# Cross attention of a decoder layer: halves prepared outside the items, value products in two passes

## The reference, cut to what matters

```python
x = layernorm(x + attn(x, W_K, W_Q, W_V, W_O))        # 16 heads, causal
x = layernorm(x + xattn(x, ctx, ctx, gamma))          # this is the stage that changes
x = layernorm(x + ffn(x, W_g, W_u, W_d))              # ternary weights

def xattn(q, k, v, gamma):        # all (4, 512, 512); 8 heads of 64 rows of the second axis
    qh, kh, vh = (t.reshape(B, 8, 64, 512) for t in (q, k, v))
    qk = einsum('bhdq,bhdl->bhql', qh, kh) / sqrt(64)
    sm = softmax(qk, axis=-1)
    return gamma * einsum('bhql,bhdl->bhdq', sm, vh).reshape(B, 512, 512)
```

## Time and profile before

| | us |
|---|---|
| median of 3 runs | 1504.17 |
| lowest and highest | 1502.49, 1505.21 |
| the profiled execution, its own time | 1502.57 |
| its span, from first to last instruction | 1500.8 |
| TensorE busy | 1434.7 (96%) |
| VectorE busy | 1100.5 (73%) |
| ScalarE busy | 725.1 (48%) |
| GpSimd busy | 636.6 (42%) |

### The profile page before, as it was taken

How to read it: one execution, slowest core, us unless ns; L and a number is a source line. 1 busy time by engine, 2 the same in 40 slices (tenths; PEclk the granted TensorE clock), 3 DMA queues, 4 the chain that set the end, 5 groups by cost and what they waited for, 6 DMA issues and landing times. The chain is left out here.

```text
span 1500.8 us, 24088 instructions
## 1 busy us (share of the span) xinstructions
PE 1434.7 (96%) x6988; PEld 1146.6 (76%) x7008; DVE 1100.5 (73%) x2368; ACT 725.1 (48%) x1549; POOL 636.6 (42%) x493
## 2 busy tenths in 40 slices
PE   7999999999999999999999999859999989999996
PEld 5788888888888888888888888737887765565564
DVE  4667677776777676777767776678999995796854
ACT  3444444545444444444353544438987863323332
POOL 1333424334243334242433433357887853343432
PEclk9999999999999999999999999979999999999998
DMA  6566666666656666666666664811224103000000
GB/s 175 155 166 169 167 169 163 167 161 166 161 164 160 161 161 171 167 165 164 162 167 158 168 166 133 210 50 54 60 60 151 36 1 112 1 29 28 0 29 28
DMA packets 193609, 185.09 MB, mean 123 GB/s; under 512 B 97057, under 2 KB 170785, under 8 KB 193313
## 3 DMA queue, kind: packets, MB, share of 16 engines
q1 hardware_dynamic: 192416, 184.09, 45.7%
q10 hardware_dynamic: 1152, 0.52, 0.2%
HBM read 113.25 MB, written 71.30 MB: 123 GB/s over the span
## 5 line engine op out<-in xcount | busy, mean ns | idle before, releaser
L583 ACT ACTIVATE probs<-probs,neg_max 128x128 f32<-128x128 f32 (+3 forms) x256 | 142.5, 557 | 357.8 <-DVE neg_max L707 350.2
L411 POOL TENSOR_TENSOR v_lo<-placed,v_hi 128x512 fp32r<-128x512 f32 x64 | 83.2, 1299 | 366.1 <-ACT v_hi L589 366.1
L413 POOL TENSOR_TENSOR pT_lo<-placed,pT_hi 128x1280 fp32r<-128x1280 f32 x64 | 189.2, 2956 | 0.0
L767 DVE SCALAR_TENSOR_TENSOR acc<-attn_bank,prob_recip,acc 128x512 f32<-128x512 f32 x256 | 174.8, 745 | 8.1 <-PE attn_bank L483 3.3
L1303 POOL TENSOR_TENSOR prod_lo<-prod,prod_hi 128x512 fp32r<-128x512 f32 x64 | 84.7, 1323 | 143.2 <-ACT prod_hi L1412 143.2
L707 DVE CUSTOM_DVE_ANT_0 probs<-attn_bank,mask 128x128 f32<-128x128 f32 (+3 forms) x256 | 117.2, 481 | 8.3
L682 DVE TENSOR_TENSOR qT_lo<-attn_bank,qT_hi 128x512 fp32r<-128x512 f32 x64 | 44.2, 691 | 105.2 <-ACT qT_hi L571 105.2
L950 POOL TENSOR_SCALAR xprobs<-xprobs,xprob_recip 128x512 f32<-128x512 f32 x128 | 99.9, 797 | 36.1 <-DVE xprob_recip L1130 36.0
L719 DVE STREAM_TRANSPOSE turned<-probs 128x256 f32<-128x256 f32 (+1 forms) x384 | 113.9, 362 | 0.0
L1362 PE MATMUL y_bank<-wdT_f32r,prod_hi 128*128 128x512 f32 x256 | 110.7, 432 | 2.3 <-POOL prod_lo L1303 1.8
L483 PE MATMUL attn_bank<-woT_hi,zT_hi 128*128 128x512 f32 x256 | 101.2, 395 | 8.9 <-DVE zT_lo L682 8.9
(11 more groups left out here) (145 smaller groups left out, 3887.5 us busy)
## 6 DMA issues: line engine op xcount, KB each, us to landing
turned_scratch<-turned SPq DMA_DIRECT2D x64, 896.0 KB, 3.9
placed<-turned_scratch SPq DMA_DIRECT2D x256, 224.0 KB, 4.3
rows_twice<-in_ctx_dram SPq DMA_DIRECT2D x64, 128.0 KB, 2.6
acc<-in_x_dram SPq DMA_DIRECT2D x16, 256.0 KB, 5.2
rows<-in_L_attn_W_V_dram SPq DMA_DIRECT2D x64, 64.0 KB, 2.3
rows<-in_L_attn_W_O_dram SPq DMA_DIRECT2D x64, 64.0 KB, 2.7
rows_twice<-in_L_ffn_W_g_dram SPq DMA_DIRECT2D x64, 64.0 KB, 3.1
rows_twice<-in_L_ffn_W_u_dram SPq DMA_DIRECT2D x64, 64.0 KB, 2.0
```

The source lines that it names most:

```text
L413: nc.gpsimd.tensor_tensor(pT[par][1][:], placed_probs, pT[par][0][:].bitcast(F32), ALU.subtract).then_inc(p_lo, 1)
L583: nc.scalar.activation(probs[:, cols], probs[:, cols], ACT.Exp, bias=low[:, par, t:t + 1], scale=-1.0, accum_out=total[:, par, t:t + 1]).t ...
L767: nc.vector.scalar_tensor_tensor(out=acc[:, b * NT + t, :], in0=s_bank[t][:], scalar=recip[:, b, t:t + 1], in1=acc[:, b * NT + t, :], op0= ...
```

## The change

In attention, the context is split into halves ahead of its use. At the end of each head's loop (step 3) SyncE loads one of the sixteen context tiles, GpSimd scales it by one eighth (`XSCALE`) and makes its high and low part (`split`, three operations of 512 columns), and SyncE writes both to DRAM (`keep_halves`, 512 KB). The load of `wu` moves from step 0 to step 1, since the tile shares a slot with it. For the last head, `split` stands in GpSimd's queue between the last `halves_lo` and the two norm powers, and SyncE waits for the last write before the stage ends.

In cross attention, SyncE loads ready halves for item m + 4 (two DMAs of 256 KB, `load_halves`). The halves of `x` are made once for a pair: ScalarE takes the high part of the 128 rows in unit 1 of even items, GpSimd the low part, and SyncE copies them from `rows_pair` into `xs` with two DMAs of 128 KB for each item. GpSimd's `split_context` and VectorE's `xs` operation are gone.

The value product of a unit is two matmuls. `val` holds five blocks of 64 columns for each pair: low of item 0, high of item 0, zeros, high of item 1, low of item 1. For item 0 the weights are (low, high) against the high probabilities and (high, zeros) against the low ones, for item 1 (high, low) and (zeros, high). So each item has a bank of its own: 64 rows hold high values by high probabilities, or with it high by low, and the other 64 the remaining part. Both must be scaled by gamma and added: ScalarE takes one half of the bank into `z_gamma` (`main_part`), VectorE adds the other (`rest`), both for each item, in unit 1 of the next item (for h = 7 at the item's end). GpSimd's addition of a pair now stands behind the scaling of the next even item, and for the last pair of a batch in item 7.

```diff
+    def load_halves(self, sp, cp, b, h):
+        for side in range(2):
+            sp.dma_start(cp[h % 2][side * XD:(side + 1) * XD, :, :],
+                         self.kept[bass.ds(b, 1), h * XD:(h + 1) * XD, :, :].rearrange("o r k d -> (o r) k d")).then_inc(self.halves_loaded[h % 2], 16)
...
                     if b == 3:
                         keep_signs(h, 0)
+                        wait_apart(sp, k, f_turn, h * 3 + 3)
+                        rows.load_split_tile(sp, h)
...
                     if b == 3:
                         keep_signs(h, 1)
                         keep_signs(h, 2)
+                        rows.keep_halves(sp, halves, k, h)
...
                 for b in range(1, B):
                     halves_lo(FIRST + b, b % 2)
+                rows.split(nc, pool, halves, k, H - 1)
                 for b in range(2):
                     norm_gpsimd(nc, pool, norm, k.minus_half, b)
...
-                    nb, nh = ahead(b, h, 6)
-                    if exists(m + 6, ITEMS) and exists(m + 4, ITEMS):
-                        wait_count(sp, cp_ready, m + 5)
-                        source.load_twice(sp, nb, nh)
+                    nb, nh = ahead(b, h, 4)
+                    if exists(m + 4, ITEMS):
+                        if exists(m + 2, ITEMS):
+                            wait_apart(sp, k, scores_full, m * NT + 3 * NT)
+                        source.load_halves(sp, cp, nb, nh)
+                        rows = slice(nh % 2 * XD, (nh % 2 + 1) * XD)
+                        if nh % 2 == 0:
+                            wait_apart(sp, k, x_lo, nb * PAIRS + (nh // 2 + 1))
+                        for part in range(2):
+                            sp.dma_start(xs[nh % 2][part * XD:(part + 1) * XD, :].bitcast(F32),
+                                         x_parts[rows, part, :]).then_inc(xs_loaded[nh % 2], 16)
                     if is_item(b, h, B - 2, 0):
                         signs.load(sp)
...
+                def pairs_to_add(b, h):
+                    pair = h // 2 - 1 if h % 2 == 0 else PAIRS - 1 if h == XH - 1 else -1
+                    return [pair] if pair >= 0 and exists(b * XH + 2 * pair, ITEMS - 2) else []
...
                             nc.gpsimd.tensor_scalar(probs[q][:, t, :], probs[q][:, t, :], recip[:, q, t:t + 1], 1.0,
                                                     ALU.mult, ALU.mult).then_inc(probs_ready, 1)
-                    if pair_ends(b, h):
-                        pool.wait_ge(z_scaled, b * PAIRS + (h // 2 + 3))
-                        tile = acc[:, bass.ds(b * NT + h // 2, 1), :].rearrange("p o d -> p (o d)")
+                    for pair in pairs_to_add(b, h):
+                        wait_apart(pool, k, z_scaled, b * XH + (2 * pair + 4))
+                        tile = acc[:, bass.ds(b * NT + pair, 1), :].rearrange("p o d -> p (o d)")
                         nc.gpsimd.tensor_tensor(tile, z_gamma[:], tile, ALU.add).then_inc(z_added, 1)
...
-                            for n, (vp, pp) in enumerate(SPLIT):
-                                lt = nc.tensor.matmul(z_bank[pair % 2][:], val[vp][:, j, pair, 2 * par:2 * par + 2, :].rearrange("p a d -> p (a d)"),
-                                                      pT[pp][:, j, :], start=(par == 0 and j == 0 and n == 0),
-                                                      stop=(par == 1 and j == NT - 1 and n == 2))
+                            for pp, slot in enumerate(((0, 1), (3, 2))[par]):
+                                lt = nc.tensor.matmul(z_bank[par][:], val[:, j, pair, slot:slot + 2, :].rearrange("p a d -> p (a d)"),
+                                                      pT[pp][:, j, :], start=(j == 0 and pp == 0), stop=(j == NT - 1 and pp == 1))
...
+                def main_part(b, h, j):
+                    g = z_turn(b, h, j)
+                    if g is None or not exists(b * XH + g, ITEMS - 2):
+                        return
+                    own, other = z_rows(g)
+                    act.wait_ge(z_full, b * XH + (g + 1))
+                    if g % 2 == 0:
+                        act.wait_ge(z_added, b * PAIRS + (g // 2 + 1))
+                    nc.scalar.activation(z_gamma[own, :], z_bank[g % 2][other, :], ACT.Copy, scale=source.gamma[other, 0:1]).then_inc(z_main, 1)
...
+                def rest(b, h, j):
...
+                    dve.wait_ge(z_main, b * XH + (g + 1))
+                    nc.vector.scalar_tensor_tensor(out=z_gamma[own, :], in0=z_bank[g % 2][own, :], scalar=source.gamma[own, 0:1],
+                                                   in1=z_gamma[own, :], op0=ALU.mult, op1=ALU.add).then_inc(z_scaled, 1)
...
+                def last_pair(g):
...
-                dve.wait_ge(z_full, B * PAIRS)
-                tile = acc[:, B * NT - 1, :]
-                nc.vector.scalar_tensor_tensor(out=tile, in0=z_bank[(PAIRS - 1) % 2][:], scalar=source.gamma[:, 0:1], in1=tile,
-                                               op0=ALU.mult, op1=ALU.add).then_inc(z_added, 1)
+                for g in (XH - 2, XH - 1):
+                    last_pair(g)
```

155 lines of the change are left out of this document (93 added, 62 removed).

## The result

| kernel | median us | lowest to highest | ratio to before, 95% |
|---|---|---|---|
| before | 1504.2 | 1502.5 to 1505.2 | |
| after | 1543.4 | 1539.9 to 1546.6 | 1.0264, 1.0245 to 1.0282 |

A forecast was written before the change was run, and what follows sets the result against it. TensorE bounds attention; in cross attention TensorE, VectorE and ScalarE stand close together, and VectorE becomes the bound. Terms for batches, stage ends, signs and start sum to +31.5 us on 1502.6, 1534.1, for the median 1536; range 1518 to 1556.

The forecast's parts named there:

- The bound of a pair: Cross attention: TensorE falls from 13.4 to 11.6 us, VectorE binds at 11.9; with 0.5 for hand-overs, 12.4 without waits.
- rival D: Value products: the two remaining matmuls take longer than two of three did, so no cut; no chance of its own.
- The wait for the addition: Cross attention: one z_gamma buffer makes VectorE's rest wait 3.0 us for GpSimd, eleven times; such pairs take 15.4.
- Rival A: Cross attention: no wait for GpSimd's addition, which ends before ScalarE's turn; 1502 us, faster than before; chance 0.12.
- The clock: Cross attention: TensorE's clock held in most waits, at nothing in the sum; up to six falls within the range.
- rival B: Cross attention: TensorE's clock falls in each of eleven waits, 1.7 us each, +19, 1555 us; chance 0.17.
- The signs: Items 16 to 18: loads for item 21 land behind the 4 MB, TensorE waits; +3.4 us, from 0 to 6.
- Batch 2: Cross attention: waits plus a norm no longer partly hidden behind the bound VectorE; 65.0 us against 58.0, +7.0.
- Batch 3: Cross attention, VectorE already the bound: two waits partly filled by norm operations, 2 x 1.2, and one rest more; +3.0 us.
- End of attention: Last head: GpSimd's split ahead of batch 0's norm power delays VectorE; +2.9 us, 0 if the engine behind has slack.
- Start of the cross stage: First scores wait for GpSimd's low part and a DMA of xs; +2.0 us, between 0 and 4.
- Rival C: Cross attention: a transfer late in every item, 28 items x 0.5 us on top of the forecast, 1550; chance 0.06.

The follow-up runs named there:

- two buffers: The changed kernel with a second z_gamma buffer, so a pair's first product waits for the addition of the pair before the last: 1513.2 us, 1.0066.
- the experiment with the addition first: The changed kernel with one z_gamma, GpSimd adding the pair ahead of its four scalings of the even item instead of behind them: 1513.0 us, 1.0059.
- the busy wait: The changed kernel with TensorE repeating a unit's transposes six times in items 3, 5 and 7 of each batch, so it hardly idles: 1537.2 us, 1.0222.
- the pieces: The changed kernel with the two 2 MB loads of signs at item 16 made eight of 512 KB, one an item from 16 to 23: 1540.3 us.
- all repairs: The changed kernel with a second z_gamma, signs in eight loads, end-of-attention edits, item 0's query cast earlier, last pair's main parts on ScalarE with one addition: 1504.8 us, 1.0005.
- the halves alone: The changed kernel's split, kept and loaded context and query halves, with value products and z as in the kernel before: 1512.7 us, 1.0059.
- the experiment on the end of attention: The changed kernel with the last context tile's split behind the first norm power and the last W_u load ahead of batch 2's exchange: 1544.1 us.

## Why the prediction was right, and where its sum was not

The forecast was 1536, with 1518 to 1556; 1543.4 came, 7 above it. The sign, the mechanism and its place were right. That the sum came as near as it did is in part luck, as the end of this list shows.

- **Attention loop**, nothing: right. TensorE is busy for 440 of 440 us beside 176 GB/s.
- **The bound of a pair**: TensorE's 11.6 and VectorE's 11.9 stand. The hand-overs were put at 0.5 and are 0.9 (12.8 in the first pair and, with two buffers, in all). The step left ScalarE out, which needs 12.4 by its pitch and is the nearest of the three. Value matmuls still start 0.23 apart, so rival D had nothing in it.
- **The wait for the addition**: the mechanism, its place and the count of eleven were right, and taking it away by a buffer or by GpSimd's order gives 30 us. Its size was 2.3, not 3.0: the addition ended 4.3 us behind the reciprocal, not 4.7, because the four scalings take 2.70 where the earlier trace rows had 3.12, and VectorE came to `rest` 2.75 behind it, not 2.6. Rival A didn't come; it would have needed the order of the experiment with the addition first, and even there the time was 1513, not 1502.
- **The clock** is the term that was mis-sized most. The sum put it at nothing, "the clock held in most", with up to six falls in its own range. Six waits of eleven were followed by half clock in the profiled execution, and the busy wait gave 6 us back, about four falls, in the median. So the truth lay between the forecast and rival B, which had all eleven. A pair with a fall is 12.8 + 2.3 + 1.6 = 16.7, one without it 15.1, where 15.4 was forecast. The price, 1.7 against 1.6, was right by luck: it took a fall of 6.8 us and half of its loss hidden by TensorE's slack; the fall lasts 3.4 us, and of the 1.7 us of work that it loses almost nothing was hidden. And the bracket, 2.94 us left alone and 4.14 followed by a fall, was drawn from two gaps of the attention stage. The trace of before had a third, the 2.64 us ahead of the first scores in the earlier trace rows, at the start of the stage, where TensorE had had little to do. Behind that one the clock fell:

```profile
996.60:997.20 0.60, 0.60 (x3) 0.51 (x4) 0.00 (x0) 0.00 (x0) 0.60 (x1) 1.00 0.64 140
997.20:1000.00 2.80, 2.80 (x9) 1.50 (x7) 2.42 (x4) 1.84 (x4) 2.80 (x3) 0.51 0.49 140
```

The Trainium skill, "TensorE: Matmul & The Clock Gate", section "A second HAM failure mode: psum-queue depth-cycling", which the prediction weighed, tells of short idle times that make the clock swing; the cross stage agrees with it, at 0.93 granted over 1036 to 1150 us, against 1.00 both with two buffers and with the busy wait.
- **The signs**: the mechanism was right, the term too small: 3.4 was put down, within 0 to 6, and the pieces gave 5.9 to 6.2 back.
- **Batch 2**: its norm was put down in full, 7.2, since VectorE is the bound. With all repairs, so without the waits, the falls and the 4 MB in one go, batch 2 takes 55.0, which is 3.8 more than four pairs of 12.8. About half of the norm is hidden after all: a pair of 12.8 leaves VectorE, at 11.9, some room.
- **Batch 3**: 3.0 was forecast, 1.4 came. Two buffers take it to 37.7, so the two waits cost 1.7 and not 2.4, and without them the batch is 0.3 faster than before where one `rest` more should have made it 0.6 slower. VectorE there is rid of more than I took off; with the halves alone the batch is 4.1 faster.
- **End of the stage**: 2.9 forecast, 3.0 measured, from four chained operations. **End of attention**: 2.9 for the split was right (979.43 to 982.19), but the stage began 5.8 later. Of the rest, 2.2 us are a later start of GpSimd's last low part, within what kernels with the same code differ by, as the experiment on the end of attention shows. From there to the stage's first transposes it is 18.6 us before and 22.2 after. About 1.1 of this difference is the clock: attention's last output products take 0.63 each in the changed kernel's execution, at half clock (granted 0.50 from 990 to 996), and 0.39 before. With two buffers, where they take 0.39 too, the way is 21.1, 2.5 more than before, and that is the term. So the 12.5 us by which the two profiled spans differ beyond the sum hold 2.2 that no run shows to be the change's.
- **Start of the cross stage**: 2.0 within 0 to 4 was forecast; TensorE's first scores are 7.8 us behind its first transposes where they were 3.7, 4.1 more. The copy of xs was priced at its own 2.6 us, but it stood behind loads of cp and raw tiles. Putting 0.5 MB of these behind it brought the first scores 2.8 us nearer, and the whole 2.3. Rival C, a transfer late in every item, didn't come: TensorE waits for `xs` twice in the stage, here and behind the signs.

The mis-sized terms go both ways. Too small were 0.4 in each of twelve pairs, the six falls of the clock (9), the signs (3) and the way to the first reciprocal (6, with the 2.2 just named), some 23 us. Too large were 0.7 in each of nine waits, the norm of batch 2 (3) and batch 3 (2), some 11 us. What is left is the 12.5 of the profiled executions, and 7 between the medians, because the profiled one is the slowest of four.

## What to carry to other kernels

A buffer that is used once a pair is safe only as long as the step that frees it stands ahead of slow work in its engine's queue: when an edit moves a use forward, look where the release stands; here swapping two blocks on GpSimd was worth 30 us. When a cut on the bound engine is planned, add up every engine's pitch for the new loop, since the second and third may be within a few per cent, and count what a wait costs TensorE afterwards. Large loads whose result is wanted late go in pieces between the small ones that are wanted now.

## What the hardware showed unexpectedly

- A TensorE gap of 2.33 us was followed by about 3 us at half clock (granted 0.50 from 1052.5 to 1055.5), while one of 2.94 in the attention stage was not the earlier trace rows. In the same cross stage a gap of 2.28 ahead of 1084.91 was not followed by a fall either (granted 1.00 from 1084.91 to 1094.34), and one of 2.15 ahead of 1215.52 was (0.77 from there to 1223). The length of the gap alone didn't decide.
- Four norm operations on VectorE (128x512 float32, from SBUF to SBUF) took 3.49 us beside GpSimd's scalings and subtraction and 1.92 without, in three kernels against one that differs from the last of them by this alone. The Trainium skill, "SBUF — State Buffer", section "SBUF: two separate sides", says that VectorE in some modes and GpSimd take turns on a shared pair of ports, the one that comes second standing still for the whole instruction. The 1.57 us more are in line with it; which instruction stood still, no row shows.
